# Last graph layer: who forms the last column group's weights and totals, and where its third T block is made

## Chip, cores and metric

One core of one Trainium2 chip. The metric is the device time of one execution in microseconds (us); the runs of the kernel before have a median of 404.36 us.

## What is computed

Four graph layers run one after the other on x (1354 rows of 256) with one dense matrix adj (1354 x 1354, many zeros). Each layer normalises its input (layer norm, then relu), forms a new term and adds it to x. Only the last layer, called layer 3, is touched by the change:

```python
def _L3_gnn_ref(x, S, W, U):
    S = S + jnp.eye(n, dtype=S.dtype)
    h = x @ W
    scores = h @ U @ h.T
    mask = S > 0
    scores = jnp.where(mask, scores, -jnp.inf)
    att = jax.nn.softmax(scores, axis=-1)
    att = att * mask.astype(att.dtype)
    S_tilde = S * att
    return S_tilde @ h
```

## The kernel before

All work is laid out transposed. The 1354 nodes make 11 blocks of 128 rows (the last one has 74). The columns of the score matrix make three groups of 512, 512 and 330. A tile n = 11 * group + row block, so there are 33 tiles, 0 to 32; tiles 22 to 32 are the last group. fp32 products are made of three matmuls, on a high part (fp32r) and the remainder below it ("hi" and "lo").

The order is written by hand, for each engine its own instruction stream, joined by semaphores. In layer 3 the streams run over steps s. For one tile the stages are:

- TensorE: score(s) (six matmuls, L324 to L326, into bank 4 or 5), for which the block T of the tile's group is needed. T is made by make_t(group): 12 matmuls on TensorE, a copy on ScalarE (t_hi_part, L532) and a subtraction on VectorE (t_lo_part, L903).
- VectorE: add3 (mask and negated score, L1387) and running (the group's elementwise minimum, L966 and L955).
- Once per group, when all 11 tiles have their scores: turn_max on TensorE (L1580), top on VectorE (L934), spread_max on TensorE (L1589). It gives each column's extreme value.
- VectorE: shift (L974) subtracts that value. ScalarE: exp3 (L842). The exponentials go into a slot in SBUF.
- The weight, exponential times adj: weights3 on GpSimd (L466), for the tiles in OWN_W (22, 24, 25, 27, 28, 30, 31) times_s on VectorE (L1396).
- The total of the exponentials over the group's tiles: add_total on GpSimd (L475 for the first sum, L478 for the others), directly behind weights3 of the same tile.
- ScalarE: w_hi (L848) writes the weight's high part, then copies the weight into PSUM bank 3 (L850). VectorE: weights3_lo (L1403) subtracts both. There is one such bank, so the copy of tile n waits for the subtraction of tile n-1. The high parts have a ring of three, so w_hi(n) waits until aggregate3(n-3) is done.
- TensorE: aggregate3(n) multiplies the weight with the values (L1894 and L1896 with the high part, L1900 with the low part): 12 matmuls of 256 columns for groups 0 and 1, 9 for group 2, each group into its own sums in PSUM. A matmul with a row of zeros (L1892) opens a bank that holds two sums.
- add_up(group) on TensorE (L1916): the totals, summed over partitions. It stands right behind the last aggregate3 of its group, and for group 2 inside aggregate3(32). Then totals_inverse (L1416) and out3 (L1426) on VectorE, and a store of each block by a DMA that SyncE issues (L376).

Shift, weight, low part and aggregate of a tile follow its score by 12, 13, 14 and 15 steps in groups 1 and 2. On VectorE step s has: shift, times_s of the tile before, weights3_lo of the tile before that; in step 37 totals_inverse(1), which waits for add_up(1); in steps 38 to 41 one out3 each. On ScalarE the order is exp3(n), w_hi(n-1), copy(n-1), exp3(n+1).

The lines that the change touches are in the GpSimd stream (weights3, add_total), the ScalarE stream (t_hi_part(2, 1), values, exp3, w_hi), the VectorE stream (times_s, out3, t_lo_part(2, 1)) and the TensorE stream (aggregate3, add_up, make_t(2, 1)).

Of the kernel before, what the change touches and what calls it, by code (L numbers as in the profile page):

```python
# [14 lines left out]
D = 256  # L15
# [67 lines left out]
SUMS3 = [[(0, 0), (0, D), (1, 0), (1, D)]] * 2 + [[(4, 0), (5, 0), (7, 0)]]  # L83
TOTALS_BANK, COPY_BANK = 2, 3
OWN_W = [n for n in range(2 * NB, NT) if n % 3 != 2]
# [6 lines left out]
T3_BANKS = [[0, 1], [6, 7], [6, 7]]  # L92
# [6 lines left out]
def graph_layers_kernel(nc, x, adjT, wq, wk, wvT, wsa, wgcn, w2, w3, w3T, u3T, asa, cols, rws, eye, out):  # L99
    with ExitStack() as ctx:  # L100
# [199 lines left out]
        w_own, w_copied = sem("w_own"), sem("w_copied")  # L300
# [6 lines left out]

        def w_done(eng, n):

            if n in OWN_W:  # L310
                eng.wait_ge(w_own, OWN_W.index(n) + 1)
            else:
                eng.wait_ge(w_set, n + 1 - sum(k < n for k in OWN_W))

# [66 lines left out]
        def _(pool):  # L381
# [97 lines left out]

            for n in range(NT):  # L480
                if n not in OWN_W:
                    weights3(n)
                add_total(n)
# [3 lines left out]
        def _(act):  # L487
# [333 lines left out]
            for s in range(NB):  # L821
                if s == 5:
                    z(8, 3)
                    z(9, 3)
                    z(10, 3)
                if 6 <= s <= 8:
                    h_hi(s + 2, 3)
                if s < 8:
                    values(s, 1)
                if s == 6:  # L830
                    t_hi_part(1, 1)
                if s < 4:
                    h_hi(s + 4, 3)
                if s < 3:
                    yT_out(s + 8)
                if s == 9:
                    t_hi_part(2, 1)
# [6 lines left out]
            def w_hi(n):  # L844

                w_done(act, n)
# [16 lines left out]
        def _(dve):  # L863
# [554 lines left out]
            def out3(b):  # L1418

                r, gi = rows(b), b // PER  # L1420
                dve.wait_ge(rinv_set[1], gi + 1)
                if gi < 2:
                    dve.wait_ge(agg[1], NB * (gi + 1))
                else:
                    dve.wait_ge(last_sum, b % PER + 1)  # L1425
                dve.scalar_tensor_tensor(out=x_sb[0:r, b, :], in0=sum3(b), scalar=rinv[0:r, b:b + 1],  # L1426
                                         in1=x_sb[0:r, b, :], op0=ALU.mult, op1=ALU.add).then_inc(x_add[3], 1)


            for s in range(NB):  # L1430
                if 1 <= s < 5:
                    h_lo(s + 3, 3)
                if 6 <= s <= 8:
                    h_lo(s + 2, 3)
                if 2 <= s < 5:
                    out2(s + 6)
                add3(s)
                running(s, 1, ALU.min)
                if s < 8:
                    values3_lo(s)  # L1440
                if s == 6:
                    t_lo_part(1, 1)
                if s == 9:
                    t_lo_part(2, 1)
# [3 lines left out]
            dve.memset(f(spare_mask[0:1, :]), 0.0)  # L1448
            values3_lo(8)
            for s in range(12, NT + LAG3 - 1):  # L1450
# [14 lines left out]
                for n in tiles_at(s, 1):  # L1465
                    if n in OWN_W:
# [17 lines left out]
        def _(pe):  # L1484
# [393 lines left out]
            def aggregate3(n):  # L1878
# [10 lines left out]
                for b in blocks(gi):  # L1889
                    if gi < 2 and j == 0 and b % 2 == 0:  # L1890
                        wait(pe, x_add[3], b - PER + 2)
                        pe.matmul(ps[:, SUMS3[gi][b % PER][0], :], g[0][0:1, 0, 0:P], spare_mask[0:1, :], start=True, stop=False)  # L1892
                    mine = slice((b % PER) * P, (b % PER) * P + rows(b))
                    pe.matmul(sum3(b), p_lo[0:k, n % RING, mine], g[0][0:k, j, 0:D], start=(gi == 2 and j == 0),  # L1894
# [3 lines left out]
                for b in blocks(gi):  # L1898
                    mine = slice((b % PER) * P, (b % PER) * P + rows(b))
                    ins = pe.matmul(sum3(b), w_lo[0:k, n % RING, mine], g[0][0:k, j, 0:D], start=False,  # L1900
                                    stop=(j == NB - 1 and (gi == 2 or b % 2 == 1)))
# [18 lines left out]
            for s in range(NT + LAG3):  # L1920
# [18 lines left out]
                if s == 9:  # L1939
# [59 lines left out]
```

## Time and profile before

| what | value |
|---|---|
| runs (three) | 404.36, 408.68, 404.33 us; median 404.36 us |
| profiled execution | 405.73 us, of which the span is 403.9 us |
| granted TensorE clock | 0.987 of full speed on average |
| busy shares | TensorE 96%, its weight loads 89%, VectorE 84%, ScalarE 63%, GpSimd 29% |
| layer 3's aggregation | from 323.3 us to the span's end |
| group 1's add-up | starts at 382.80 us |
| last reciprocal | starts at 398.76 us |
| last output block | 399.76 us, then 0.77 us until its store is issued and the rest of the span for landing |

The profile lists instructions with their start and length in us from the span's start. On VectorE, ScalarE and GpSimd an instruction's listed length overlaps the start of the next one a little, so the difference of two neighbouring starts is what one costs in a busy row of them. Matmuls are pipelined: a 256-column matmul is listed with 0.28 us, and in a dense row the next one starts 0.12 us later.

### The profile page before, as it was taken

What the parts mean: (1) busy time and instruction counts of PE and PEld (TensorE: products, weight loads), DVE (VectorE), ACT (ScalarE), POOL (GpSimd) and SP (SyncE); (2) the same over time, 40 slices, a digit from 0 to 9 for tenths busy, and PEclk for the clock granted to TensorE, in tenths of its full rate; (3) what the DMA queues carried; (4) which work ended last, traced back from release to release, by engine and by line L of the source; (5) the groups of instructions that cost most, each with busy time, mean ns of one, the idle gap of its engine ahead of it and who ended that gap; (6) DMA issues with size and microseconds to landing.
All of it is one profiled execution on the core that took longest, in us unless ns stands there. A gap on an engine that the chain in (4) does not pass through costs nothing. (4 is left out here: it accounts for less than half of the span.)

```text
span 403.9 us, 7765 instructions
## 1 busy us (share of the span) xinstructions
PE 388.6 (96%) x2651; PEld 357.7 (89%) x2651; DVE 339.2 (84%) x772; ACT 252.7 (63%) x529; POOL 118.9 (29%) x131
## 2 busy tenths in 40 slices
PE   8999999999799999999999989999999899999894
PEld 6788888999699899999899989999888789989794
DVE  4898899899786757999999989765897889699894
ACT  2554699888677576787588794245332366357772
POOL 1290000001010243332023011051010398469982
PEclk9999999999989999999999999999999999999988
DMA  8994000000000001000000000000000000010011
GB/s 254 376 379 142 0 0 2 2 0 2 0 2 0 2 1 54 2 1 2 3 0 2 2 2 2 0 2 0 2 2 0 0 2 2 0 54 1 2 53 35
DMA packets 10319, 13.98 MB, mean 35 GB/s; under 512 B 661, under 2 KB 7209, under 8 KB 10281
## 3 DMA queue, kind: packets, MB, share of 16 engines
q1 hardware_dynamic: 9736, 12.96, 9.4%
q10 hardware_dynamic: 544, 0.52, 0.4%
q8 instruction: 22, 0.36, 0.4%
q14 instruction: 17, 0.13, 0.1%
HBM read 12.10 MB, written 1.39 MB: 33 GB/s over the span
## 5 line engine op out<-in xcount | busy, mean ns | idle before, releaser
L1602 PE MATMUL ps<-v_hi,p_hi 128*128 128x258 f32 (+3 forms) x242 | 64.7, 298 | 1.5 <-DVE s_sb L1207 1.2
L391 POOL TENSOR_TENSOR mr_all<-mr_all,mhalf 128x4 f32<-128x4 f32 (+1 forms) x12 | 13.1, 1089 | 167.8 <-DVE mr_all L888 167.8
L1603 PE MATMUL ps<-v_lo,p_hi 128*128 128x258 f32 (+3 forms) x242 | 61.4, 283 | 0.0
L1602 PEld LDWEIGHTS ps<-v_hi,p_hi 128*128 128x128 f32 (+3 forms) x242 | 45.1, 186 | 3.3 <-issue 1.8
L1603 PEld LDWEIGHTS ps<-v_lo,p_hi 128*128 128x128 f32 (+3 forms) x242 | 45.1, 186 | 0.6
L1607 PE MATMUL ps<-v_hi,p_lo 128*128 128x258 f32 (+3 forms) x242 | 40.5, 286 | 1.1 <-DVE p_lo L1171 1.1
L974 DVE TENSOR_TENSOR s_sb<-s_sb,ps 128x512 f32<-128x512 f32 (+3 forms) x63 | 38.4, 610 | 0.8 <-PE ps L1589 0.7
L428 POOL TENSOR_TENSOR mid_lo<-adjT_sb,mid_hi 128x512 fp32r<-128x512 f32 (+2 forms) x16 | 20.1, 1258 | 51.0 <-ACT mid_hi L663 51.0
L1607 PEld LDWEIGHTS ps<-v_hi,p_lo 128*128 128x128 f32 (+3 forms) x242 | 32.8, 186 | 1.8 <-DVE p_lo L1171 1.6
L1894 PE MATMUL ps<-big_hi,p_lo 128*128 128x256 f32 (+3 forms) x121 | 32.7, 299 | 0.6 <-ACT p_lo L848 0.5
L1602 PE MATMUL ps<-big_hi,mid_hi 128*128 128x258 f32 (+3 forms) x121 | 31.7, 293 | 0.0
L1896 PE MATMUL ps<-big_lo,p_lo 128*128 128x256 f32 (+3 forms) x121 | 31.3, 287 | 0.0
L1603 PE MATMUL ps<-big_lo,mid_hi 128*128 128x258 f32 (+3 forms) x121 | 30.3, 282 | 0.0
L672 ACT ACTIVATE p_hi<-s_sb,minus_r 128x512 fp32r<-128x512 f32 (+3 forms) x33 | 22.1, 670 | 11.6 <-PE ps L1607 6.2
L1164 DVE SCALAR_TENSOR_TENSOR s_sb<-s_sb,sx 128x512 f32<-128x512 f32 (+3 forms) x33 | 25.7, 778 | 1.2
L324 PE MATMUL ps<-mid_hi,big_hi 128*128 128x512 f32 (+3 forms) x66 | 25.4, 384 | 0.6 <-DVE mid_lo L907 0.6
L980 DVE TENSOR_TENSOR p_lo<-s_sb,p_hi 128x512 fp32r<-128x512 f32 (+3 forms) x33 | 20.5, 622 | 6.2 <-ACT s_sb L551 5.9
L550 ACT ACTIVATE p_hi<-s_sb 128x512 fp32r<-128x512 f32 (+3 forms) x33 | 19.0, 577 | 10.6 <-DVE s_sb L974 10.3
L1894 PEld LDWEIGHTS ps<-big_hi,p_lo 128*128 128x128 f32 (+3 forms) x121 | 23.1, 191 | 2.7 <-ACT p_lo L848 1.3
L324 PE MATMUL ps<-mid_hi,v_hi 128*128 128x512 f32 (+3 forms) x66 | 25.3, 383 | 0.0
L842 ACT ACTIVATE s_sb<-s_sb 128x512 f32<-128x512 f32 (+3 forms) x30 | 17.2, 574 | 12.6 <-DVE s_sb L974 12.5
L966 DVE TENSOR_TENSOR m_sb<-m_sb,s_sb 128x512 f32<-128x512 f32 (+3 forms) x36 | 24.2, 672 | 0.7
(251 smaller groups left out, 1230.8 us busy)
## 6 DMA issues: line engine op xcount, KB each, us to landing
adjT_sb<-in_adjT_dram SPq DMA_DIRECT2D x1, 2816.0 KB, 16.5
adjT_sb<-in_adjT_dram SPq DMA_DIRECT2D x3, 768.0 KB, 9.1
adjT_sb<-in_adjT_dram SPq DMA_DIRECT2D x1, 1815.0 KB, 20.9
out_dram<-x_sb SPq DMA_DIRECT2D x10, 128.0 KB
x_sb<-in_x_dram SPq DMA_DIRECT2D x2, 256.0 KB, 3.5
x_sb<-in_x_dram SPq DMA_DIRECT2D x1, 512.0 KB, 3.7
adjT_sb<-in_adjT_dram SPq DMA_DIRECT2D x1, 512.0 KB, 11.4
rows_sb<-in_rows_dram SPq DMA_DIRECT2D x1, 385.0 KB, 11.4
```

Of the source, the lines that this page charges most:

```text
L324: eng.matmul(out_ap, lhs[0], rhs[0], start=first, stop=False)
L428: pool.tensor_tensor(adj_ring(at[1], n), adj_tile_b(n), f(adj_ring(at[0], n)), ALU.subtract).then_inc(alo_odd, 1)
L672: act.activation(ring(p_hi, n), sum1(n), ACT.Exp, bias=bias, scale=SLOPE - 1.0).then_inc(e_hi, 1)
L966: dve.tensor_tensor(m, m, mine(n), op).then_inc(s_max[a], 1)
L974: dve.tensor_tensor(mine(n), mine(n), ps[0:rows(j), bank, 0:CW[gi]], ALU.subtract).then_inc(s_sub[a], 1)
L980: dve.tensor_tensor(ring(p_lo, n), slot(n), f(ring(p_hi, n)), ALU.subtract).then_inc(plo, 1)
L1164: dve.scalar_tensor_tensor(out=sum1(n), in0=left[0:rows(j), gi, 0:CW[gi]], scalar=sx[0:rows(j), j, 0:1], in1=sum1(n), op0=ALU.add, op1=ALU ...
L1602: pe.matmul(out_ap, left_[0][0:k, n % RING, mine], right_[0][0:k, j, 0:cols_], start=(j == 0), stop=False)
L1603: pe.matmul(out_ap, left_[0][0:k, n % RING, mine], right_[1][0:k, j, 0:cols_], start=False, stop=False)
L1607: ins = pe.matmul(ps[0:rows(b), banks[b % PER], 0:cols_], left_[1][0:k, n % RING, mine], right_[0][0:k, j, 0:cols_], start=False, stop=(j ...
L1894: pe.matmul(sum3(b), p_lo[0:k, n % RING, mine], g[0][0:k, j, 0:D], start=(gi == 2 and j == 0), stop=False)
L1896: pe.matmul(sum3(b), p_lo[0:k, n % RING, mine], g[1][0:k, j, 0:D], start=False, stop=False)
```

## The change

- GpSimd forms the weights of all 11 tiles of group 2; OWN_W, times_s and the semaphore w_own go.
- The totals of tiles 19, 20 and 21 (the last three of group 1) come three weights later on GpSimd: behind weights3 of tiles 22, 23 and 24.
- Of group 2's totals GpSimd adds tiles 27, 29 and 31 only (two additions). VectorE adds the other eight in PSUM bank 7 (one copy, seven additions, in the place where times_s stood but behind weights3_lo), and adds both halves at the end (join_totals).
- The sums of output blocks 9 and 10 share bank 5, so bank 7 is free. A matmul with zeros opens bank 5. In aggregate3 of group 2 the low-part matmuls go in the order 8, 10, 9. The last add-up waits for join_totals.
- make_t(2, 1) moves from step 9 to step 11 and stands between turn_max(0) and spread_max(0), its banks become 0 and 3; values(8) goes behind spread_max(0). t_hi_part(2, 1) and t_lo_part(2, 1) follow, and the memset of spare_mask moves ahead to step 9. ScalarE's first exp3, values and w_hi come in a new order, written out by hand.

```diff
-SUMS3 = [[(0, 0), (0, D), (1, 0), (1, D)]] * 2 + [[(4, 0), (5, 0), (7, 0)]]
-TOTALS_BANK, COPY_BANK = 2, 3
-OWN_W = [n for n in range(2 * NB, NT) if n % 3 != 2]
+SUMS3 = [[(0, 0), (0, D), (1, 0), (1, D)]] * 2 + [[(4, 0), (5, 0), (5, D)]]
+TOTALS_BANK, COPY_BANK, LAST_TOTAL_BANK = 2, 3, 7
+POOL_TOTALS = [2 * NB + 5, 2 * NB + 7, 2 * NB + 9]
...
-T3_BANKS = [[0, 1], [6, 7], [6, 7]]
+T3_BANKS = [[0, 1], [6, 7], [0, 3]]
...
+            def add_last_total(n):
+
+                k = POOL_TOTALS.index(n)
+                pool.wait_ge(pf[1], n + 1)
+                pool.wait_ge(tot_add, 2 * NB - 3 + k)
+                r = totals[0][0:rows(n % NB), 0:CW[2]]
+                if k == 1:
+                    pool.wait_ge(tot_mm, 1)
+                pool.tensor_tensor(r, r if k > 1 else slot3(POOL_TOTALS[0]), slot3(n), ALU.add).then_inc(tot_add, 1)
+
             for n in range(NT):
-                if n not in OWN_W:
-                    weights3(n)
-                add_total(n)
+                weights3(n)
+                if n < 2 * NB - 3:
+                    add_total(n)
+                elif 2 * NB <= n < 2 * NB + 3:
+                    add_total(n - 3)
+                elif n in POOL_TOTALS[1:]:
+                    add_last_total(n)
...
+            t_hi_part(2, 1)
             values(8, 1)
-            for n in range(NT):
+            exp3(0)
+            values(9, 1)
+            exp3(1)
+            act.wait_ge(t_lo[1], 2 * NG)
+            w_hi(0)
+            values(10, 1)
+            for n in range(2, NT):
                 exp3(n)
-                if n < 2:
-                    values(n + 9, 1)
-                if n:
-                    w_hi(n - 1)
+                w_hi(n - 1)
             w_hi(NT - 1)
...
-            def times_s(n):
-
+            def last_totals(n):
+
+                j, r = n - 2 * NB, ps[0:rows(n % NB), LAST_TOTAL_BANK, 0:CW[2]]
                 dve.wait_ge(pf[1], n + 1)
-                dve.wait_ge(phi, NT + n - 2)
-                dve.wait_ge(w_copied, n - 2)
-                dve.tensor_tensor(full3(n), slot3(n), adj_tile(n), ALU.mult).then_inc(w_own, 1)
+                if j == 0:
+                    dve.tensor_copy(r, slot3(n)).then_inc(last_total, 1)
+                else:
+                    dve.wait_ge(last_total, j - sum(k < n for k in POOL_TOTALS))
+                    dve.tensor_tensor(r, r, slot3(n), ALU.add).then_inc(last_total, 1)
+
+            def join_totals():
+
+                dve.wait_ge(last_total, NB - len(POOL_TOTALS))
+                dve.wait_ge(tot_add, 2 * NB)
+                dve.tensor_tensor(totals[0][:, 0:CW[2]], ps[:, LAST_TOTAL_BANK, 0:CW[2]], totals[0][:, 0:CW[2]], ALU.add).then_inc(last_total, 1)
...
             add3(11)
             top(0, 1, ALU.min)
             shift(0, 1)
-            dve.memset(f(spare_mask[0:1, :]), 0.0)
+            t_lo_part(2, 1)
             values3_lo(8)
...
-                for n in tiles_at(s, 1):
-                    if n in OWN_W:
-                        times_s(n)
                 for n in tiles_at(s, 2):
                     weights3_lo(n)
+                for n in tiles_at(s, 1):
+                    if n >= 2 * NB and n not in POOL_TOTALS:
+                        last_totals(n)
...
+            join_totals()
             totals_inverse(2)
...
-                if s == 9:
-                    make_t(2, 1)
-                if s == 11:
-                    pe.wait_ge(t_lo[1], 2 * NG)
-                    turn_max(0, 1)
+                if s == 11:
+                    pe.wait_ge(t_lo[1], 2 * C)
+                    turn_max(0, 1)
+                    make_t(2, 1)
+                    spread_max(0, 1)
                     values(8, 1)
-                    spread_max(0, 1)
```

How the streams stand. First GpSimd from the weight of tile 19 on; a product with adjT_sb is a weight, a sum into raw_b is a total of group 1, one into raw_a a total of group 2. Before:

```order
L466 TENSOR_TENSOR z_buf<-s_sb,adjT_sb 128x512
L478 TENSOR_TENSOR raw_b<-raw_b,s_sb 128x512
L466 TENSOR_TENSOR asa_sb<-s_sb,adjT_sb 128x512
L478 TENSOR_TENSOR raw_b<-raw_b,s_sb 128x512
L466 TENSOR_TENSOR z_buf<-s_sb,adjT_sb 74x512
L478 TENSOR_TENSOR raw_b<-raw_b,s_sb 74x512
L466 TENSOR_TENSOR asa_sb<-s_sb,adjT_sb 128x330
L475 TENSOR_TENSOR raw_a<-s_sb 128x330
L478 TENSOR_TENSOR raw_a<-raw_a,s_sb 128x330 x2
```

The same place now:

```order
L459 TENSOR_TENSOR z_buf<-s_sb,adjT_sb 128x512
L459 TENSOR_TENSOR asa_sb<-s_sb,adjT_sb 128x512
L459 TENSOR_TENSOR z_buf<-s_sb,adjT_sb 74x512
L459 TENSOR_TENSOR z_buf<-s_sb,adjT_sb 128x330
L471 TENSOR_TENSOR raw_b<-raw_b,s_sb 128x512
L459 TENSOR_TENSOR asa_sb<-s_sb,adjT_sb 128x330
L471 TENSOR_TENSOR raw_b<-raw_b,s_sb 128x512
L459 TENSOR_TENSOR z_buf<-s_sb,adjT_sb 128x330
L471 TENSOR_TENSOR raw_b<-raw_b,s_sb 74x512
L459 TENSOR_TENSOR z_buf<-s_sb,adjT_sb 128x330
```

Group 1's last total (raw_b, 74x512) used to stand behind the weight of tile 21; it now stands behind the weight of tile 24. TensorE's add_up(1) and VectorE's totals_inverse(1) stand where they stood.

Then VectorE around totals_inverse(1), with the semaphores waited for, before (steps 36 to 38; the product into z_buf is times_s):

```order
L974 TENSOR_TENSOR s_sb<-s_sb,ps 128x330 [waits s_max1,mb_mm1]
L1396 TENSOR_TENSOR z_buf<-s_sb,adjT_sb 128x330 [waits w_copied,phi,pf1]
L1403 TENSOR_TENSOR w_lo<-ps,p_lo 128x330 [waits agg1,w_copied,phi]
L1416 RECIPROCAL rinv<-ps 128x4 [waits tot_mm]
L974 TENSOR_TENSOR s_sb<-s_sb,ps 128x330 [waits s_max1,mb_mm1]
L1396 TENSOR_TENSOR z_buf<-s_sb,adjT_sb 128x330 [waits w_copied,phi,pf1]
L1403 TENSOR_TENSOR w_lo<-ps,p_lo 128x330 [waits agg1,w_copied,phi]
L1426 SCALAR_TENSOR_TENSOR x_sb<-ps,rinv,x_sb 128x256 [waits agg1,rinv_set1]
```

And now (L983 is shift, L1421 weights3_lo, L1408 a total into bank 7, L1434 totals_inverse, L1444 out3):

```order
L983 TENSOR_TENSOR s_sb<-s_sb,ps 128x330 [waits s_max1,mb_mm1]
L1421 TENSOR_TENSOR w_lo<-ps,p_lo 128x330 [waits agg1,w_copied,phi]
L1408 TENSOR_TENSOR ps<-ps,s_sb 128x330 [waits last_total,pf1]
L1434 RECIPROCAL rinv<-ps 128x4 [waits tot_mm]
L983 TENSOR_TENSOR s_sb<-s_sb,ps 128x330 [waits s_max1,mb_mm1]
L1421 TENSOR_TENSOR w_lo<-ps,p_lo 128x330 [waits agg1,w_copied,phi]
L1408 TENSOR_TENSOR ps<-ps,s_sb 128x330 [waits last_total,pf1]
L1444 SCALAR_TENSOR_TENSOR x_sb<-ps,rinv,x_sb 128x256 [waits agg1,rinv_set1]
```

Each step has lost a product of two SBUF operands ahead of the low part and has a sum with one PSUM operand behind it. The shifts of tiles 26 and on stand behind the reciprocal in both.

## Rows read from the trace of the kernel before

**Rows 1.** The page: busy time of each engine over the span.

```profile
PE 388.6 (96%) x2651; PEld 357.7 (89%) x2651; DVE 339.2 (84%) x772; ACT 252.7 (63%) x529; POOL 118.9 (29%) x131
```

**Rows 2.** Windows late in the span: busy us per engine, then granted clock, DMA share, GB/s.

```profile
365.00:370.00 5.00, 5.00 (x40) 5.00 (x39) 4.79 (x10) 3.58 (x7) 5.00 (x5) 1.00 0.01 2
...
380.00:385.00 5.00, 4.21 (x28) 3.80 (x28) 4.83 (x7) 4.29 (x10) 4.26 (x5) 0.85 0.00 0
385.00:390.00 5.00, 5.00 (x37) 5.00 (x36) 5.00 (x15) 4.35 (x11) 3.69 (x5) 0.81 0.16 54
```

**Rows 3.** Timeline of TensorE, steps 9 to 14: start, length, instruction, idle before.

```profile
309.80 0.31 PE L324 MATMUL ps<-v_hi,wa_hi 128*128 128x330 f32 x1
...
311.63 0.39 PE L324 MATMUL ps<-mid_hi,v_hi 128*74 128x512 f32 x1
...
314.77 0.63 PE L1580 MATMUL ps<-ident,m_sb 128*128 128x128 f32 x4 [0.20 <-DVE m_sb L966]
...
316.55 0.65 PE L1589 MATMUL ps<-ident,mx 128*128 128x128 f32 x4 [0.43 <-DVE mx L934]
...
323.32 0.47 PE L1892 MATMUL ps<-spare_mask,big_hi 1*128 1x512 f32 x1 [0.55 <-issue]
```

**Rows 4.** Timeline of VectorE in the same stretch.

```profile
313.21 0.68 DVE L1387 SCALAR_TENSOR_TENSOR s_sb<-adjT_sb,ps 74x512 f32<-74x512 f32 x1 [0.40 <-PE ps L326]
...
322.81 0.41 DVE L1410 TENSOR_TENSOR big_lo<-ps,big_hi 74x256 fp32r<-74x256 f32 x1
```

**Rows 5.** Timeline of GpSimd, weight of tile 19 to first weight of group 2.

```profile
373.89 1.30 POOL L466 TENSOR_TENSOR z_buf<-s_sb,adjT_sb 128x512 f32<-128x512 f32 x1
375.12 1.31 POOL L478 TENSOR_TENSOR raw_b<-raw_b,s_sb 128x512 f32<-128x512 f32 x1
376.39 1.09 POOL L466 TENSOR_TENSOR asa_sb<-s_sb,adjT_sb 128x512 f32<-128x512 f32 x1
...
378.68 1.28 POOL L466 TENSOR_TENSOR z_buf<-s_sb,adjT_sb 74x512 f32<-74x512 f32 x1
379.93 1.27 POOL L478 TENSOR_TENSOR raw_b<-raw_b,s_sb 74x512 f32<-74x512 f32 x1
```

**Rows 6.** Timeline of ScalarE: exponentials 20 and 21, w_hi(25), then exponential and copy.

```profile
374.97 0.63 ACT L842 ACTIVATE s_sb<-s_sb 128x512 f32<-128x512 f32 x1 [1.11 <-DVE s_sb L974]
...
376.62 0.64 ACT L842 ACTIVATE s_sb<-s_sb 74x512 f32<-74x512 f32 x1
...
386.08 0.48 ACT L848 ACTIVATE p_lo<-z_buf 128x330 fp32r<-128x330 f32 x1
...
388.42 0.48 ACT L842 ACTIVATE s_sb<-s_sb 128x330 f32<-128x330 f32 x1
...
389.24 0.45 ACT L850 ACTIVATE ps<-z_buf 128x330 f32<-128x330 f32 x1
```

**Rows 7.** Timeline: add-ups of groups 1 and 2, last low part, last reciprocal.

```profile
382.80 1.06 PE L1916 MATMUL ps<-ones,raw_b 128*128 128x1 f32 x8
...
397.30 0.50 DVE L1403 TENSOR_TENSOR w_lo<-ps,p_lo 74x330 fp32r<-74x330 f32 x1 [0.57 <-ACT ps L850]
...
398.76 0.18 DVE L1416 RECIPROCAL rinv<-ps 128x3 f32<-128x3 f32 x1 [0.96 <-PE ps L1916]
```

**Rows 8.** Groups by shape from 380 us on: count, busy us, mean ns, idle before.

```profile
L1396 DVE TENSOR_TENSOR z_buf<-s_sb,adjT_sb 128x330 f32<-128x330 f32 x7 | 6.5, 936 | 0.0
...
L466 POOL TENSOR_TENSOR asa_sb<-s_sb,adjT_sb 128x330 f32<-128x330 f32 x3 | 2.7, 886 | 1.2 <-ACT s_sb L842 1.2
```

**Rows 9.** Timeline of VectorE in step 39: low part, out3 between, next shift.

```profile
387.10 0.49 DVE L1403 TENSOR_TENSOR w_lo<-ps,p_lo 128x330 fp32r<-128x330 f32 x1
...
387.90 0.48 DVE L974 TENSOR_TENSOR s_sb<-s_sb,ps 128x330 f32<-128x330 f32 x1
```

**Rows 10.** Line L1396: shortest, median and longest duration in ns.

```profile
L1396 DVE TENSOR_TENSOR z_buf<-s_sb,adjT_sb x7: 489/1028/1832, 379.7 to 394.8; 128x330 f32<-128x330 f32 x7
```

**Rows 11.** The chain that ended last: what one matmul of 256 columns adds to it.

```profile
395.35 0.12 PE ps L1894
```

More of the change, by code:

```diff
@@ L299, in graph_layers_kernel @@
         eye_add, w_set, tot_add, tot_mm, last_sum = (sem(n) for n in ("eye_add", "w_set", "tot_add", "tot_mm", "last_sum"))
-        w_own, w_copied = sem("w_own"), sem("w_copied")
+        last_total, w_copied = sem("last_total"), sem("w_copied")
         def wait(eng, s, value):
@@ L306, in wait @@
                 eng.wait_ge(s, value)
-        def w_done(eng, n):
-            if n in OWN_W:
-                eng.wait_ge(w_own, OWN_W.index(n) + 1)
-            else:
-                eng.wait_ge(w_set, n + 1 - sum(k < n for k in OWN_W))
         def h_done(eng, layer, count):
@@ L835, in _ @@
                     yT_out(s + 8)
-                if s == 9:
-                    t_hi_part(2, 1)
             def exp3(n):
@@ L844, in w_hi @@
             def w_hi(n):
-                w_done(act, n)
+                act.wait_ge(w_set, n + 1)
                 wait(act, agg[1], n - 2)
@@ L1424, in out3 @@
                 else:
-                    dve.wait_ge(last_sum, b % PER + 1)
+                    dve.wait_ge(last_sum, 1 if b == 2 * PER else NB - 2 * PER)
                 dve.scalar_tensor_tensor(out=x_sb[0:r, b, :], in0=sum3(b), scalar=rinv[0:r, b:b + 1],
@@ L1443, in _ @@
                 if s == 9:
-                    t_lo_part(2, 1)
+                    dve.memset(f(spare_mask[0:1, :]), 0.0)
             add3(11)
@@ L1464, in _ @@
                         shift(n, 1)
-                for n in tiles_at(s, 1):
-                    if n in OWN_W:
-                        times_s(n)
                 for n in tiles_at(s, 2):
                     weights3_lo(n)
+                for n in tiles_at(s, 1):
+                    if n >= 2 * NB and n not in POOL_TOTALS:
+                        last_totals(n)
                 if s == 24:
@@ L1884, in aggregate3 @@
                     pe.wait_ge(vlo, 2 * NB)
+                    pe.wait_ge(t_lo[1], 2 * NG)
                     h_done(pe, 3, NB)
@@ L1889, in aggregate3 @@
                 for b in blocks(gi):
-                    if gi < 2 and j == 0 and b % 2 == 0:
-                        wait(pe, x_add[3], b - PER + 2)
+                    paired = b != 2 * PER
+                    if paired and j == 0 and b % 2 == (gi == 2):
+                        if gi == 1:
+                            pe.wait_ge(x_add[3], b - PER + 2)
                         pe.matmul(ps[:, SUMS3[gi][b % PER][0], :], g[0][0:1, 0, 0:P], spare_mask[0:1, :], start=True, stop=False)
                     mine = slice((b % PER) * P, (b % PER) * P + rows(b))
-                    pe.matmul(sum3(b), p_lo[0:k, n % RING, mine], g[0][0:k, j, 0:D], start=(gi == 2 and j == 0),
+                    pe.matmul(sum3(b), p_lo[0:k, n % RING, mine], g[0][0:k, j, 0:D], start=(not paired and j == 0),
                               stop=False)
@@ L1897, in aggregate3 @@
                 pe.wait_ge(plo, NT + n + 1)
-                for b in blocks(gi):
+                for b in (8, 10, 9) if gi == 2 else blocks(gi):
                     mine = slice((b % PER) * P, (b % PER) * P + rows(b))
                     ins = pe.matmul(sum3(b), w_lo[0:k, n % RING, mine], g[0][0:k, j, 0:D], start=False,
-                                    stop=(j == NB - 1 and (gi == 2 or b % 2 == 1)))
+                                    stop=(j == NB - 1 and (b % 2 == 1 or b == 2 * PER)))
                     if n == NT - 1:
@@ L1909, in add_up @@
             def add_up(gi):
-                pe.wait_ge(tot_add, 10 * (gi + 1))
+                if gi < 2:
+                    pe.wait_ge(tot_add, 10 * (gi + 1))
+                else:
+                    pe.wait_ge(last_total, NB - len(POOL_TOTALS) + 1)
                 if gi:
@@ L1938, in _ @@
                     make_t(1, 1)
-                if s == 9:
+                if s == 11:
+                    pe.wait_ge(t_lo[1], 2 * C)
+                    turn_max(0, 1)
                     make_t(2, 1)
-                if s == 11:
-                    pe.wait_ge(t_lo[1], 2 * NG)
-                    turn_max(0, 1)
+                    spread_max(0, 1)
                     values(8, 1)
-                    spread_max(0, 1)
                 if 12 <= s < 14:
```

## Prediction

> **What bounds the kernel now.** I read the page's busy shares first [rows 1], then the windows of the last 40 us [rows 2], then the timelines of each engine. The reader is to see that TensorE is the bound nearly everywhere (388.6 us busy of 403.9), so that only two kinds of change can help: one that closes a gap on TensorE, or one in the tail, where it is no longer the bound. There are two such places. Around steps 11 to 14 TensorE waits three times, 0.20, 0.43 and 0.55 us, for the group minimum, for its reduction and before the first aggregate [rows 3]. From 380 us on the bound passes to VectorE: 5.00 of 5.00 us busy in the window from 385 [rows 2], while TensorE is busy 4.21 of 5 in the window before it. GpSimd is a third party: 5.00 of 5.00 between 365 and 370 [rows 2], a weight and a total in turns. Its last total of group 1 starts at 379.93 and takes 1.27 [rows 5]; TensorE's add-up of that group follows at 382.80 [rows 7]. So that total had 1.6 us to spare and no more.
>
> The sum is made in the profiled execution (405.73 us, span 403.9) as a difference, and the difference is put onto the median of the runs, 404.36 us.
>
> **Part 1, the third T block into the turn.** Nothing is added on TensorE; 12 matmuls (311.63 - 309.80 = 1.83 us) [rows 3] go from ahead of scores 10 and 11 to behind turn_max. Without them score 10 is ready 1.8 us earlier. VectorE still has its own work ahead, and a memset of 0.4 now; I let add3(10) start at 311.75 instead of 313.21 [rows 4]. Turn_max followed it by 314.77 - 313.21 = 1.56, so it comes at 313.3. TensorE is then busy 0.4 with it and 1.83 with T, to 315.55, while VectorE adds, reduces and is done before that (by the same offset of 3.34 from add3(10) to spread_max, at 315.1). Spread_max starts at 315.55 instead of 316.55 [rows 3], and waits for nothing. Then come 0.7 us of values(8) that stood ahead of it, so score 12 gains only 0.3. What counts is the first aggregate: it waited for the low part of values(10), which VectorE started at 322.81 [rows 4] and for which TensorE stood 0.55 us [rows 3]. VectorE's stream from shift(0) on starts 1.0 earlier, less two subtractions of 0.41 for T that now stand there, plus 0.4 for the memset that left: 0.6 to 0.7. From there to the last scores TensorE is full and carries this along. I take **-0.7 us**; bounds: 0 if ScalarE's new order delays the values, -1.2 if all three gaps (0.20 + 0.43 + 0.55) close.
>
> **Part 2, group 1's add-up.** Here I expect the cost. On GpSimd three totals of group 1 move behind three weights of group 2 each, but TensorE's add_up(1) and VectorE's totals_inverse(1) have not moved, and they wait for the last of them. GpSimd step by step, in the time of the trace before: weight 19 from 373.89 for 1.23 [rows 5]; weight 20 can start when its exponential is done, 374.97 + 0.53 = 375.5 [rows 6], and takes 1.05 (its listed 1.09 less the overlap) [rows 5], to 376.6; weight 21 after the exponential at 376.62 + 0.6, to 378.5. Exponential 22 moves up a little and ends at 378.65, since ScalarE no longer waits for weight 20 at 377.5. From 378.7 GpSimd runs through weight 22, total 19, weight 23, total 20, weight 24, total 21: three weights of 0.86 (886 ns listed [rows 8]) and three totals of 1.27 [rows 5], 6.4 us, to 385.1. TensorE has aggregate 21 behind it at 380.9 (weight 21's low part comes 1.1 us earlier than before) and stands still until 385.1. The add-up starts **2.35 us late** (385.15 against 382.80). Queued behind it on TensorE are all aggregates of group 2; on VectorE, behind the reciprocal that waits for the add-up, the shift of tile 26 and with it every later exponential. The weights up to 24, which are ready, help nobody, because the high parts have a ring of three and w_hi(25) waits for aggregate 22.
>
> **Part 3, the way back.** After 385.15: add-up 1.0 (listed 1.06 [rows 7]); the new matmul with zeros 0.3 (0.47 listed [rows 3]); aggregate 22, nine matmuls of 0.12 [rows 11], 1.1. So w_hi(25) starts at 387.6 instead of 386.08 [rows 6]: 1.5 late. From w_hi(25) to the start of the last low part it took 397.30 - 386.08 = 11.2 us before [rows 6, 7], 11.7 to its end. Now the seven products on VectorE (6.5 us [rows 8]) are gone and seven sums and a copy come in, 8 x 0.41 = 3.3 us, but the interval isn't shortened by that difference. One round is now: the copy frees the low part, then low part, total, out3, shift (0.40 each, by (387.90 - 387.10) / 2 [rows 9]), then the exponential; 1.7 us where a step has both total and out3 (steps 39 and 41), 1.3 with one of them (40 and 43). ScalarE alone needs three instructions, 0.41 each by (389.24 - 388.42) / 2 [rows 6], 1.25 with the hand-over, in the other three. That is 2 x 1.7 + 2 x 1.3 + 3 x 1.25 = 9.75; with the last copy and low part (0.95) and 0.5 in which weight 32 waits behind GpSimd's total of tile 31, 11.2 us to the end of the last low part. This gives back 0.5. The join of both totals stands between the last low part and the last add-up; TensorE used to find the totals ready, now it waits about 0.3. Sum for parts 2 and 3 at full clock: 1.5 - 0.5 + 0.3 = **+1.3 us**. Bounds: GpSimd's narrow weights, of which three were measured [rows 8], a tenth shorter or longer give -0.3 and +0.3 on the start, the low parts' hand-over -0.5 and +0.5.
>
> **Part 4, TensorE's clock.** Before, waits that left TensorE 4.21 of 5 us busy were followed by a granted clock of 0.85 and 0.81 in the two windows from 380 to 390, that is (0.15 + 0.19) x 5 x 2 = 3.4 us at 1.2 instead of 2.4 GHz [rows 2]. I price it at nothing there, because VectorE was the bound. Now TensorE stands for 4.2 us without a matmul, so I expect the fall again, and right where everybody waits for TensorE: the add-up at half speed costs 1.0 more, and if the slow stretch covers aggregate 22 as well, another 1.1. Bounds 0 and +2.4; I take **+1.0 us**, the stretch of before in its old place.
>
> The Trainium skill, TensorE: Matmul & The Clock Gate, Part 1: The HAM clock gate, says that the throttled state is the default and that activity lifts it, so an idle engine falls back. Rows 2 agree with it; by it this term wouldn't be 0.
>
> The other edits: two sums in bank 5 and the order 8, 10, 9 change only when the last two blocks may be read, and VectorE's own out3 of block 8 (0.47) covers that; nothing. The eight totals in bank 7 touch no bank that another engine uses then; nothing beyond the 0.41 each.
>
> **Sum.** -0.7 + 1.3 + 1.0 = +1.6 us: 404.36 + 1.6 = **406.0 us**, slower by 0.4%. A change under 2% is about what a measurement of this kernel can't tell from none. The forecast's own range: -1.2 + 1.3 - 0.3 + 0 gives 404.2; 0 + 1.3 + 0.3 + 2.4 gives 408.4 us.
>
> **Rivals.**
> A. The late total is absorbed: parts 2 and 3 come out at nothing, because VectorE was full anyway and the lighter steps win back the whole 2.35 us. For it: VectorE at 5.00 of 5.00 from 385 on [rows 2]. Against it: it waits itself, with tile 26's shift behind its reciprocal. 404.36 - 0.7 = 403.7 us.
> B. The products on VectorE were the whole tail. They take from 489 to 1832 ns for the same shape [rows 10], the long ones while GpSimd is in one of its own; a sum with a PSUM operand doesn't show that (0.48 [rows 9]). Then 6.5 - 3.3 = 3.2 us less, join 0.4 more, and part 1: 404.36 - 2.8 - 0.7 = 400.9 us. It needs group 1's total not to be waited for, against the order of the streams. The Trainium skill, GPSIMD Engine Reference, section 1 (Specifications), says that GpSimd shares its SBUF interfaces with VectorE and that they contend when VectorE has two SBUF inputs. Rows 10 agree, and by that rule alone this rival would be the forecast.
> C. The clock stays down. If TensorE remains at 1.2 GHz through group 2, it is the bound again: from 385.15 an add-up of 2.0, zeros 0.6, eleven aggregates of 9 x 0.24 = 2.16 (23.8), a last add-up 1.0, so the last reciprocal comes at 412.5 instead of 398.76, 13.8 later; less part 1, 404.36 + 13.1 = 417.5 us. It decides from about the third slow aggregate on, from where each costs 2.16 less a round of 1.4. Against it: before, the clock was back after 3.4 us of dense matmuls [rows 2].
> D. The change doesn't do what it says in part 1: values(8) to (10) come too late for the first aggregate, gain 0. 404.36 + 2.3 = 406.7 us.
>
> **Chances.** Forecast 0.56, D 0.13, A 0.17, B 0.10, C 0.04. The range for 8 in 10 takes in A and D and the forecast's own bounds, and leaves out B and C: 402.8 to 408.4 us. Faster by over 2% (under 396.3) has no case of its own, 0.01; slower by over 2% (over 412.4) is most of C, 0.03; within 2% 0.96.
>
> **What would show it.** Right: GpSimd's last sum into raw_b starts near 383 (383.8 less the 0.7 of part 1); TensorE has one gap of about 4 us ahead of the add-up from raw_b; the reciprocal of group 1 comes 2 to 3 us after VectorE's last instruction; a granted clock of 0.5 behind it; spread_max(0) with no wait in front, and the first matmul with zeros near 322.6. Wrong: no such gap (then A or B), or a first matmul with zeros at 323.3 or later (D), or 256-column matmuls 0.21 apart after 390 (C).

## The result

The changed kernel takes 409.33 us (median of 17 runs, 408.72 to 410.0), the kernel before 405.51 us in its 17 runs by then. The ratio is 1.0075, 95% interval 1.005 to 1.0099: slower by 3.0 us of 404.4. By the two medians it is 3.8 us, by the two means 3.1, since 5 of the 17 runs of the kernel before took 408.6 to 409.0 us and the other twelve 404.2 to 406.1. The forecast was slower by 1.6 us, 406.0, with a range up to 408.4. The direction and the place were right; the size was about half, and the time lies outside the range.

The profiled execution takes 409.0 us with a span of 407.1, 3.2 us more than before.

The page of the changed kernel, busy time of each engine (to be read against [rows 1]):

```profile
PE 389.0 (96%) x2652; PEld 357.7 (88%) x2652; DVE 337.3 (83%) x774; ACT 251.5 (62%) x529; POOL 116.9 (29%) x130
```

Every engine but TensorE has less to do, GpSimd too, and TensorE has one matmul more. The time is not work, it is waiting. The windows late in the span say where (columns as in [rows 2]):

```profile
380.00:385.00 5.00, 1.40 (x9) 1.20 (x8) 2.80 (x7) 2.80 (x7) 4.90 (x6) 0.92 0.00 0
385.00:390.00 5.00, 5.00 (x21) 4.34 (x21) 2.19 (x6) 1.14 (x3) 0.89 (x1) 0.50 0.08 26
390.00:395.00 5.00, 5.00 (x40) 5.00 (x39) 4.55 (x12) 3.66 (x10) 2.62 (x4) 0.90 0.16 54
```

Between 380 and 385 only GpSimd is full (4.90). Then TensorE is called busy for all of 5 us, but with 21 matmuls instead of 37, at a granted clock of 0.50 (1.2 instead of 2.4 GHz), while the other three hardly work. The timeline of TensorE around group 1's add-up (start, length, idle time before and who ended it; compare [rows 7]):

```profile
379.94 0.69 PE L1922 MATMUL ps<-big_hi,w_lo 74*128 74x256 f32 x4
384.23 1.86 PE L1941 MATMUL ps<-ones,raw_b 128*128 128x1 f32 x8 [3.60 <-POOL raw_b L471]
385.95 0.56 PE L1916 MATMUL ps<-big_hi,p_lo 128*128 128x256 f32 x1
```

Aggregate 21 ends at 380.63 (379.94 + 0.69) and the add-up starts at 384.23, after 3.60 us without a matmul. It takes 1.86 us instead of 1.06. GpSimd's timeline shows what it waited for (compare [rows 5]):

```profile
376.63 2.30 POOL L459 TENSOR_TENSOR z_buf<-s_sb,adjT_sb 74x512 f32<-74x512 f32 x2 [0.56 <-ACT s_sb L847]
378.89 1.28 POOL L471 TENSOR_TENSOR raw_b<-raw_b,s_sb 128x512 f32<-128x512 f32 x1
380.13 0.76 POOL L459 TENSOR_TENSOR asa_sb<-s_sb,adjT_sb 128x330 f32<-128x330 f32 x1
380.85 1.26 POOL L471 TENSOR_TENSOR raw_b<-raw_b,s_sb 128x512 f32<-128x512 f32 x1
382.08 0.87 POOL L459 TENSOR_TENSOR z_buf<-s_sb,adjT_sb 128x330 f32<-128x330 f32 x1
382.92 1.25 POOL L471 TENSOR_TENSOR raw_b<-raw_b,s_sb 74x512 f32<-74x512 f32 x1
```

Three totals and two weights stand between weight 22 and the end of the last total, without a pause. VectorE and ScalarE wait behind it: the reciprocal for the add-up, then exponential 26 for its shift, then w_hi(25) for aggregate 22 (compare [rows 6]):

```profile
386.13 0.18 DVE L1434 RECIPROCAL rinv<-ps 128x4 f32<-128x4 f32 x1 [3.26 <-PE ps L1941]
```

```profile
386.74 0.48 ACT L847 ACTIVATE s_sb<-s_sb 128x330 f32<-128x330 f32 x1 [2.94 <-DVE s_sb L983]
389.34 0.48 ACT L853 ACTIVATE p_lo<-z_buf 128x330 fp32r<-128x330 f32 x1 [2.12 <-PE ps L1922]
```

**Where the 3.2 us of the two profiles are.** The traces can't be laid on each other from zero: long before the change, at the same four matmuls of layer 2, the changed kernel is already 1.37 us ahead (286.26 against 287.63 us). So I measure between marks. Mark A is those matmuls, mark B the first matmul with zeros, mark C the four low-part matmuls ahead of turn_max(2) (start of L1922, before L1900), mark D the last reciprocal.

| stretch | before | after | difference |
|---|---|---|---|
| start to A | 287.63 | 286.26 | -1.37, not of the change |
| A to B (part 1) | 35.69 | 35.09 | -0.60 |
| B to C | 50.19 | 51.46 | +1.27 |
| C to D (the tail) | 25.25 | 29.12 | +3.87 |

Marks A and C of the kernel before, from TensorE's timeline (B is 323.32 in [rows 3], D 398.76 in [rows 7]):

```profile
287.63 1.03 PE L1849 MATMUL ps<-raw_a,m_sb 128*128 128x256 f32 x4
...
373.51 0.64 PE L1900 MATMUL ps<-big_hi,w_lo 128*128 128x256 f32 x4
```

The marks of the changed kernel, A and B on TensorE and D on VectorE (C is at 372.81 us, the same four matmuls, now of line 1922):

```profile
286.26 1.03 PE L1868 MATMUL ps<-raw_a,m_sb 128*128 128x256 f32 x4
...
321.35 0.46 PE L1914 MATMUL ps<-spare_mask,big_hi 1*128 1x512 f32 x1 [0.15 <-ACT p_lo L853]
```

```profile
401.93 0.18 DVE L1434 RECIPROCAL rinv<-ps 128x3 f32<-128x3 f32 x1 [0.83 <-PE ps L1941]
```

B to C is longer because the granted clock was 0.85 and 0.81 in the two windows from 350 to 360 us, where the profile of before has 1.00:

```profile
350.00:355.00 5.00, 4.83 (x31) 4.36 (x30) 3.83 (x9) 2.57 (x5) 2.23 (x2) 0.85 0.01 4
355.00:360.00 5.00, 5.00 (x26) 3.96 (x25) 4.41 (x9) 2.73 (x6) 3.89 (x5) 0.81 0.32 104
```

The kernel before has such a stretch at 110 to 114 us instead. Each kernel below was profiled once; e1, e2 and e5 have it at 353 like this one, the others near 110, none at both. B to C is 50.2 us in all that have it near 110, 51.5 us in all that have it at 353, whatever the edit. So I put the 1.27 us down to the execution.

### The profile page after: what moved, and what is told of

Its sections match the earlier page's. It is cut to its first block and busy times, and to the rows that moved or that the text cites. A ratio compares the mean times of both kernels' runs of the same rounds, so it can differ in the third digit from the quotient of the medians.

```text
span 407.1 us, 7769 instructions
## 1 busy us (share of the span) xinstructions
PE 389.0 (96%) x2652; PEld 357.7 (88%) x2652; DVE 337.3 (83%) x774; ACT 251.5 (62%) x529; POOL 116.9 (29%) x130
## 5 line engine op out<-in xcount | busy, mean ns | idle before, releaser
L983 DVE TENSOR_TENSOR s_sb<-s_sb,ps 128x512 f32<-128x512 f32 (+3 forms) x63 | 38.6, 613 | 1.3 <-PE ps L1608 1.3
L459 POOL TENSOR_TENSOR z_buf<-s_sb,adjT_sb 128x512 f32<-128x512 f32 (+2 forms) x20 | 21.5, 1073 | 29.9 <-ACT s_sb L847 29.8
L557 ACT ACTIVATE p_hi<-s_sb 128x512 fp32r<-128x512 f32 (+3 forms) x33 | 19.0, 577 | 11.4 <-DVE s_sb L983 11.2
L1421 DVE TENSOR_TENSOR w_lo<-ps,p_lo 128x512 fp32r<-128x512 f32 (+3 forms) x33 | 20.5, 622 | 6.7 <-ACT p_lo L853 3.7
```

The source lines that it names most:

```text
L459: pool.tensor_tensor(full3(n), slot3(n), adj_tile(n), ALU.mult).then_inc(w_set, 1)
L983: dve.tensor_tensor(mine(n), mine(n), ps[0:rows(j), bank, 0:CW[gi]], ALU.subtract).then_inc(s_sub[a], 1)
L1421: dve.tensor_tensor(ring(w_lo, n), ps[0:rows(n % NB), COPY_BANK, 0:CW[n // NB]], f(ring(p_lo, n)), ALU.subtract).then_inc(plo, 1)
```

## The experiments

The changed kernel was run 17 times, each of the others 12 times, beside the kernel before, in several sessions; between these the median of the kernel before went from 405.3 to 406.0 us, so the ratio compares better than the median. C to D is read from each one's profile, of which there is one per kernel.

| kernel | median, us | ratio to before | 95% interval | add-up from raw_b starts | C to D |
|---|---|---|---|---|---|
| changed | 409.33 | 1.0075 | 1.005 to 1.0099 | 384.23 | 29.12 |
| e1, totals back | 405.27 | 0.9983 | 0.9953 to 1.0013 | 381.08 | 24.59 |
| e2, add-up late | 404.49 | 0.9953 | 0.9926 to 0.9981 | 384.92 | 24.62 |
| e3, part 1 alone | 404.88 | 0.9978 | 0.9952 to 1.0005 | 381.95 | 25.26 |
| e4, TensorE kept busy | 406.58 | 1.0015 | 0.999 to 1.004 | 384.18 | 27.04 |
| e5, e1 and total 31 behind | 405.58 | 0.9986 | 0.9962 to 1.001 | 380.94 | 24.53 |
| e6, e2 and total 31 behind | 404.31 | 0.9979 | 0.9954 to 1.0004 | 384.71 | 24.62 |
| e7, two weights late | 407.56 | 1.0035 | 1.0008 to 1.0062 | 382.76 | 28.05 |
| e8, e3 with the late add-up | 403.83 | 0.9947 | 0.9922 to 0.9972 | 385.07 | 24.47 |
| e9, e3 with 6 spare matmuls | 404.95 | 0.9991 | 0.997 to 1.0011 | 381.93 | 25.26 |
| e10, e3 with late out3 | 404.30 | 0.9956 | 0.9935 to 0.9977 | 382.02 | 24.78 |

**e1_totals_back: the late totals undone.**

```diff
-                if n < 2 * NB - 3:
+                if n < 2 * NB:
                     add_total(n)
-                elif 2 * NB <= n < 2 * NB + 3:
-                    add_total(n - 3)
```

> The changed kernel, with one thing undone: group 1's last three totals stand behind their own weights on GpSimd again. Theory (the late total holds TensorE and VectorE): the add-up from raw_b starts about 2 us after aggregate 21 at most, the 4.3 us gap ahead of it shrinks to 1.5 us or less, the slow clock behind it is one stretch or none, and the kernel is 3 to 4 us faster than the changed one, within 1 us of the kernel before. Rival (the cost is GpSimd's seven more weights and the join at the end): the gap may shrink but the time stays within 1 us of the changed kernel, since the weights are late one by one.

Measured: 405.27 us, 4.1 less than the changed kernel. GpSimd still forms all weights of group 2 and VectorE still adds eight totals. The add-up follows aggregate 21 directly, with no idle time of TensorE shown ahead of it:

```profile
380.50 0.74 PE L1920 MATMUL ps<-big_hi,w_lo 74*128 74x256 f32 x4
381.08 0.95 PE L1939 MATMUL ps<-ones,raw_b 128*128 128x1 f32 x8
```

The granted clock is 1.00 from C to D. The theory holds, its rival falls: seven more weights on GpSimd cost nothing here.

**e2_addup_late: the late totals kept, the waiting moved.**

```diff
-                    if n == 2 * NB - 1:
+                    if n == 2 * NB + 2:
                         add_up(1)
...
-                if s == 37:
+                if s == 40:
                     totals_inverse(1)
-                if 38 <= s < 42:
-                    out3(s - 34)
+                if 41 <= s < 45:
+                    out3(s - 37)
```

> The changed kernel, with add_up(1) moved behind aggregate 24 on TensorE, totals_inverse(1) to step 40 and its four out3 to steps 41 to 44 on VectorE. GpSimd's order is untouched, so the last total of group 1 is as late as in the changed kernel. Theory: nobody waits for it any more, no gap over 1 us in front of the add-up, and the time is 4 us below the changed kernel and 0.5 to 1.5 us below the kernel before. Rival (GpSimd itself is the bound of the tail): the gap moves elsewhere and the time stays within 1 us of the changed kernel.

Measured: 404.49 us, 4.8 less than the changed kernel and faster than the kernel before (0.9953, interval up to 0.9981). GpSimd's last total of group 1 is as late as in the changed kernel, and the add-up is even later; nobody is held:

```profile
382.93 1.26 POOL L471 TENSOR_TENSOR raw_b<-raw_b,s_sb 74x512 f32<-74x512 f32 x1
```

```profile
384.92 0.95 PE L1941 MATMUL ps<-ones,raw_b 128*128 128x1 f32 x8
```

So the total itself had time. What cost was that the two engines asked for it ahead of work that didn't need it. The rival, GpSimd as the bound of the tail, falls: it is idle between weights from 385.8 on. (This edit moves the four out3 as well; e10 shows below that they alone can be worth 0.5 us.)

**e3_part1_alone: the kernel before with the T block moved.**

```diff
-                if s == 9:
-                    make_t(2, 1)
...
                     turn_max(0, 1)
-                    values(8, 1)
+                    make_t(2, 1)
                     spread_max(0, 1)
+                    values(8, 1)
```

> The kernel before, with the move of the third T block alone (banks 0 and 3, made between turn_max(0) and spread_max(0), ScalarE's new opening). Theory: the first matmul with zeros comes 0.6 to 0.7 us earlier relative to the scores of step 8, and the kernel is 0.7 us faster than before. Rival: the tail is bound by VectorE and the earlier start is given back there, 0.0 us.

Measured: ratio 0.9978 (0.9952 to 1.0005), that is 0.9 us less, with an interval that touches 1. Its profile has spread_max(0) with no wait ahead (0.43 before [rows 3]) and the tail as before (25.26 against 25.25 us), so the earlier start isn't given back there:

```profile
313.06 0.63 PE L1582 MATMUL ps<-ident,m_sb 128*128 128x128 f32 x4 [0.64 <-DVE m_sb L968]
...
315.37 0.60 PE L1591 MATMUL ps<-ident,mx 128*128 128x128 f32 x4
...
322.44 0.47 PE L1895 MATMUL ps<-spare_mask,big_hi 1*128 1x512 f32 x1 [0.16 <-ACT p_lo L846]
```

The wait ahead of turn_max(0) grew from 0.20 to 0.64 us, the two behind it shrank from 0.43 and 0.55 to none and 0.16. The sum of the waits falls by 0.38 by these rows. A to B is 35.02 us here, 0.67 less than before; the rest of that lies in what the profile doesn't call idle.

**e4_keep_busy: the clock by itself.** 34 matmuls of no use, into a part of bank 2 that nobody reads.

```diff
                     if n == 2 * NB - 1:
+                        for _ in range(34):
+                            pe.matmul(ps[:, TOTALS_BANK, 0:D], g[0][:, 0, 0:P], g[0][:, 0, 0:D], start=True, stop=True)
                         add_up(1)
```

> The changed kernel, with 34 matmuls of 256 columns of no use (4.1 us) ahead of add_up(1), into a part of bank 2 that nobody reads: TensorE is as late as before but not idle. Theory of the clock: the granted clock stays at 1.00 through the stretch behind the add-up, and the kernel is 2 to 3 us faster than the changed one, though the last total is as late. Rival (the slow clock hides behind the other engines): within 0.5 us of the changed kernel.

Measured: 406.58 us, 2.75 less than the changed kernel, though it does more work and its add-up starts as late (384.18 against 384.23; C lies 0.38 earlier). Windows of e4:

```profile
380.00:385.00 5.00, 5.00 (x46) 5.00 (x44) 2.42 (x6) 2.49 (x6) 4.64 (x5) 1.00 0.00 0
385.00:390.00 5.00, 5.00 (x40) 4.63 (x40) 4.29 (x12) 2.75 (x7) 1.67 (x2) 1.00 0.10 31
```

The clock stays at 1.00, and C to D is 27.04 instead of 29.12 us. These 2.08 us are less than the clock's whole price, because the spare matmuls run until the add-up starts and hold it a little themselves:

```profile
380.10 4.24 PE L1986 MATMUL ps<-big_hi 128*128 128x256 f32 x34
384.18 0.95 PE L1941 MATMUL ps<-ones,raw_b 128*128 128x1 f32 x8
```

From C the add-up starts at 11.75 us here and at 11.42 in the changed kernel, 0.33 later (0.1 of it because GpSimd ends its total later). From the add-up to D it takes 399.47 - 384.18 = 15.29 us here and 401.93 - 384.23 = 17.70 there. So of the tail's 3.87 us, 2.4 are the slow clock and 1.5 the wait. The rival, a clock hidden behind the other engines, falls.

**e7_delay_two: the dose.** The totals two weights late instead of three.

```diff
-                elif 2 * NB <= n < 2 * NB + 3:
-                    add_total(n - 3)
+                elif 2 * NB - 1 <= n < 2 * NB + 2:
+                    add_total(n - 2)
```

> The changed kernel with group 1's last three totals two weights late instead of three. Theory (the order on GpSimd alone sets the add-up): the last of them ends one weight of 0.75 to 0.9 us earlier, the add-up from raw_b starts 0.9 us earlier (384.23 becomes 383.3, if the last scores end at the same time), and the kernel is 0.8 to 1.0 us faster than the changed one if the slow clock has the same length, 2 to 3 us faster if it is one stretch shorter. Rival (a threshold, all or nothing): equal to the changed kernel or equal to e1.

Measured: 407.56 us, 1.8 less than the changed kernel. The last total starts at 381.44 and the add-up at 382.76, 1.0 earlier from C than in the changed kernel (10.46 against 11.42):

```profile
381.44 1.26 POOL L471 TENSOR_TENSOR raw_b<-raw_b,s_sb 74x512 f32<-74x512 f32 x1
```

```profile
382.76 1.87 PE L1941 MATMUL ps<-ones,raw_b 128*128 128x1 f32 x8 [2.63 <-POOL raw_b L471]
```

The wait shrinks from 3.60 to 2.63 us, by one weight and a hand-over, and C to D by 1.07. Its slow clock is as long as in the changed kernel (382.3 to 389.1). The median fell by more, 1.8; a part of that is that 8 of the changed kernel's 17 runs had a mean granted clock of 0.978 and none of these twelve was under 0.984. With no, two and three weights in front of the totals the tail is 24.59 (e1), 28.05 and 29.12 us: most of the cost is there with two already, since the slow clock comes as long with a gap of 2.6 us as with one of 3.6, and the third adds its own length.

**e5_last_total_behind and e6_both_late: the last total of group 2.**

```diff
-                elif n in POOL_TOTALS[1:]:
+                elif n == POOL_TOTALS[1]:
                     add_last_total(n)
+            add_last_total(POOL_TOTALS[2])
```

> e1_totals_back with one more change: GpSimd's total of tile 31 behind the weight of tile 32 instead of ahead of it. In e1 the weight of tile 32 waited 0.86 us behind that total (392.94 to 393.80) while its exponential was done. Theory (the last tile's weight is on the path that ends): the last reciprocal comes 0.4 to 0.8 us earlier, 0.5 us less than e1. Rival (VectorE's low parts and ScalarE set the end): 0.0 us.

> e2_addup_late with the total of tile 31 behind the weight of tile 32 as in e5. Theory: 0.5 us less than e2 and 1.5 us below the kernel before, the fastest of all. Rival: no better than e5, because aggregates 22 to 25 do not wait for anything in either.

Measured: C to D is 24.53 in e5 (24.59 in e1) and 24.62 in e6 (24.62 in e2). Both expectations of 0.5 us failed. (The edit shown is that of e5; e6 keeps the late totals of group 1.) In e5 GpSimd's weight of tile 32 no longer stands behind the total, and starts no earlier for it, since it now waits for its exponential:

```profile
393.59 0.89 POOL L459 TENSOR_TENSOR asa_sb<-s_sb,adjT_sb 74x330 f32<-74x330 f32 x1 [0.74 <-ACT s_sb L846]
```

My expectation said that the exponential was done all the while; in e1 it ran from 393.16 to 393.64 and the weight started at 393.80, so the total held the weight by 0.2 us at most. The rest of the round (shift, exponential, weight, high part) sets when the last weight comes; which engine's turn binds there was not tested.

**e8_before_addup_late: the kernel before, with part 1 and the late add-up.** The edit of e2 on e3: VectorE's products, GpSimd's totals and the banks are those of the kernel before.

> e3_part1_alone with add_up(1), totals_inverse(1) and its out3 moved as in e2; products and totals stay as in the kernel before. Before, TensorE waited 0.8 us ahead of aggregate 21 and 0.5 us in it, but not for the total. Theory (in this version VectorE's products bind the tail, not the add-up): within 0.3 us of e3. Rival (any late add-up is won time): 0.8 us less than e3.

Measured: 403.83 us, ratio 0.9947 (0.9922 to 0.9972), the lowest ratio of all, and 1.0 us below e3, which was run in another session. The rival was right and my theory wrong. The tail is 24.47 instead of 25.26 us. It is as short as with the new split of weights and totals (24.62 in e2), so with the late add-up that split, the largest part of the change, wins nothing that can be seen here. With add-up and out3 in their old places it may win something: e1 has the new split and 24.59 us, e3 the old one and 25.26. But e3 has the slow clock from 383 to 387 and e1 has not, and the ratios of the two (0.9983 and 0.9978) show no difference, so this 0.7 us of one profile each stays unexplained.

**e9_part1_busy and e10_out3_late: what e8 won by.** e9 puts 6 spare matmuls into a wait of TensorE; e10 moves only the four out3 on VectorE.

```diff
+                if n == 2 * NB - 1:
+                    for _ in range(6):
+                        pe.matmul(ps[:, TOTALS_BANK, 0:D], g[0][:, 0, 0:P], g[0][:, 0, 0:D], start=True, stop=True)
                 pe.wait_ge(phi, NT + n + 1)
```

```diff
-                if 38 <= s < 42:
-                    out3(s - 34)
+                if 41 <= s < 45:
+                    out3(s - 37)
```

> e3_part1_alone with 6 matmuls of no use (0.7 us) in the wait of 0.8 us ahead of aggregate 21. It asks whether the slow clock from 383 to 387 costs the kernel before anything, which the prediction put at nothing. Theory 1 (VectorE binds there, the clock costs nothing): the slow stretch goes or moves, and the time stays within 0.3 us of e3, the tail from the last aggregate of 512 columns ahead of turn_max(2) to the last reciprocal at 25.3 us. Theory 2 (e8 won by losing the slow stretch): the tail falls to 24.5 us as in e8 where the clock stays at 1.00.

> e3_part1_alone with the four out3 of blocks 4 to 7 in steps 41 to 44 on VectorE instead of 38 to 41; add_up(1) and totals_inverse(1) stay where they were. It parts the two things that e8 moved. Theory 1 (VectorE's order is what e8 won by): the tail from the last aggregate of 512 columns ahead of turn_max(2) to the last reciprocal is 24.5 us as in e8, against 25.3 in e3, though the slow clock from 383 to 387 may stay. Theory 2 (the add-up's place or the clock it brings): the tail stays at 25.3 us.

Measured: in e9 the slow stretch stayed where it was (a granted clock of about 0.5 from 383 to 387) and C to D is 25.26 us. The spare matmuls fill the wait ahead of aggregate 21; the one inside it (0.34 us) is still there. That says nothing on what the slow clock costs in the kernel before, since it never went; no experiment answers that question. The run lists give a hint. Executions of the kernel before with a mean granted clock of 0.998 or 0.999 lost about 0.8 us of it (0.002 x 402.5), too little for a stretch of 3.4 us at half speed, which loses 1.7; they took 404.2 to 404.5 us. Those at 0.987, as in the profile, took 405.5 to 406.1, some 1.5 us more. A stretch at 353 alone is worth 1.3 us by B to C, so the one at 383 costs a few tenths at most; that is an estimate. e10 has C to D at 24.78 us and a ratio of 0.9956 (0.9935 to 0.9977), with the slow stretch still there. So 0.5 of e8's 0.8 us come from VectorE's order alone: in steps 38 to 41 it has no room (5.00 of 5.00 [rows 2]), right behind steps 43 and 44 it waits for ScalarE (0.57 us twice in e3). The other 0.3 belong to the add-up's place or the clock, untested apart.

## Why the prediction was right in kind and wrong in size

**What bounds the kernel.** Right for TensorE, half right for VectorE in the tail. e10 shows that VectorE's order counts there (0.5 us). But its load is not the whole of it: from 380 to 390 us VectorE is busy 9.7 us in e8 and 8.2 in e2, and the tail is the same.

**Part 1 (-0.7 us).** Right: -0.60 between marks A and B (-0.67 in e3), and -0.9 us by e3's ratio, whose interval reaches from 0.2 us slower to 1.9 faster. Turn_max(0) came where the walk had it (its wait became longer, spread_max's vanished). The carry to the end held: e3's tail is that of before.

**Part 2, group 1's add-up.** Right, mechanism and size. From mark C to the add-up it is 9.29 us before and 11.42 after, 2.13 late where the walk said 2.35. The gap of TensorE, the order of GpSimd's six instructions, VectorE's wait at the reciprocal (3.26 us) and ScalarE's at w_hi(25) are all there. e1 and e2 take the wait away, each in its own way, and the tail falls to 24.6 us; e7 shortens it and the tail follows.

**Part 3, the way back.** Right in size, +1.5 us at full clock instead of +1.3, in part because two errors met. The piece from the add-up to w_hi(25) was short: 387.00 - 384.18 = 2.82 us in e4, where I had summed 2.45. I had put the add-up 0.2 us too late. Together w_hi(25) comes 1.7 us late (2.13 + 2.82 - 3.28, the last being 386.08 - 382.80 of the kernel before), not 1.5. The other piece, from w_hi(25) to the end of the last low part, was predicted at 11.2 us and measured at 11.2 (387.00 to 398.23), and the join costs the 0.3 that I took. In e4:

```profile
387.00 0.48 ACT L853 ACTIVATE p_lo<-z_buf 128x330 fp32r<-128x330 f32 x1 [0.74 <-PE ps L1922]
```

```profile
397.73 0.50 DVE L1421 TENSOR_TENSOR w_lo<-ps,p_lo 74x330 fp32r<-74x330 f32 x1 [0.26 <-issue]
```

**Part 4, TensorE's clock: the step that failed.** I took +1.0 us, "the stretch of before in its old place", with a bound of +2.4. It measured +2.4 (2.41 us between add-up and D, e4 against the changed kernel), my upper bound. The slow stretch was not the one of before. It lasted from 384.2 to 391.0 us, 6.8 instead of 3.4. It covered the add-up, the matmul with zeros and aggregate 22, for which ScalarE waited with w_hi(25), and aggregate 23: 389.34 - 384.23 = 5.11 us from the add-up to w_hi(25), against 2.82 at full clock. The mechanism was right. The point value counted the add-up alone and was taken from a place with shorter waits: 4.21 of 5 us busy before, 1.40 of 5 now. The sum with the measured terms is -0.6 + 1.5 + 2.4 = +3.3 us; the two profiles differ by 3.2, the ratio says 3.0.

**The base.** The forecast was put onto the median of three runs, 404.36 us. With more runs the kernel before stands at 405.5. In the run lists all its executions from 404.2 to 404.5 us have a mean granted clock of 0.998 or 0.999, those from 405.5 to 406.1 have 0.982 to 0.990 (the profile that I summed in has 0.987), and those over 408 have 0.974 to 0.979. So I added a difference of one kind of execution to the time of another. With the measured ratio, 404.36 us would be 407.4, inside the range; with the medians it is outside. The range had no room for this, and it also left out part 3's own +0.5; with that its end would have been 408.9.

**The rivals.** A (absorbed) fell: of the late start only 0.5 us came back. B (VectorE's products were the whole tail) fell, and not only because of the add-up: with that wait taken away (e1, e2) the tail is 24.6 us, at most 0.7 less than before and not 3.2, and with the products kept (e8) 24.5. That the time of the long products, up to 1832 ns, turns into waits of VectorE fits its busy times in e8 and e2; it was not tested by itself. C (the clock stays down) fell, though the stretch doubled. D fell by e3.

## What to carry to other kernels

A result that is moved later on its producer must also be asked for later. Look for every instruction that waits for it, and for what stands behind that instruction on its own engine without needing it; moving the consumers here was worth 4.8 us (e2), while the new split of weights and totals won 0.7 us of the tail at most (e1 against e3). The gap on TensorE cost twice here, 1.5 us as a wait and 2.4 as a slow clock behind it, and the second part could not be sized by a slow stretch that had shorter waits ahead. A forecast belongs onto runs of the same granted clock as the profile that it is summed in. Where one engine is full for a few steps and has room in later ones, work without a consumer nearby can go into the later steps; for the four out3 here that gave 0.5 us (e10).

## What was unexpected in the hardware

- The slow clock behind a gap had two lengths. Behind waits that left TensorE 4.21 of 5 us busy it lasted 3.4 us, behind the gap of 3.6 us it lasted 6.8 us (granted clock 0.60 in the window from 384 to 385, 0.50 until 391), and behind e7's gap of 2.6 us 6.8 us too. These windows of 1 us of the changed kernel show its beginning and its end:

```profile
384.00:385.00 1.00, 0.77 (x4) 0.77 (x4) 0.00 (x0) 0.00 (x0) 0.90 (x2) 0.60 0.00 0
...
390.00:391.00 1.00, 1.00 (x7) 1.00 (x6) 0.76 (x2) 0.55 (x2) 0.37 (x1) 0.50 0.00 0
391.00:392.00 1.00, 1.00 (x10) 1.00 (x10) 0.95 (x3) 0.75 (x2) 0.40 (x1) 0.99 0.02 8
```

- Thirty-four matmuls of no use made the changed kernel 2.75 us faster (e4), by keeping the clock up. The Trainium skill, TensorE: Matmul & The Clock Gate, Part 1: The HAM clock gate, says that activity lifts the throttle, and e4's granted clock of 1.00 agrees.
- A short slow stretch of about 3.4 us comes in every profile at one of two places, near 110 or 353 us; e2 and e6, which differ in one late total only, have it at different ones. Two executions can differ by this alone, and by more: the kernel before took from 404.2 us (mean granted clock 0.998) to 409.2 us (0.974).
